# Writing out the loops of a two-layer cross-attention kernel

## What is computed

```
layer 0:  x += cproj(attention_16_heads_of_32(LN(x), ctx, mask))
          x += proj(gelu_tanh(fc(LN(x))))               # 512 -> 2048 -> 512
layer 1:  for i in (1, 2):                               # two attentions, 16 heads of 128
              k, v = ctx @ wk_i + bk_i, ctx @ wv_i + bv_i  # and one extra key and value per head
              x += wo_i(softmax(LN(x) @ wq_i @ k.T / sqrt(128)) @ v)
          x += fc2(gelu(fc1(LN(x))))
```

## Time and profile before

| | us |
|---|---|
| median of three runs | 2413.54 (2409.4 to 2414.35) |
| profiled execution | 2421.03 |
| its span, first to last instruction | 2419.1 |
| PE busy | 2326.3 (96%) |
| PE weight loads busy | 2116.8 (88%) |
| DVE busy | 1343.4 (56%) |
| ACT busy | 1147.9 (47%) |
| POOL busy | 377.6 (16%) |

### The profile page before, as it was taken

One profiled execution on the slowest core, in us unless ns is written; L12 is line 12 of the kernel. 1 busy time (PEld: TensorE's weight loads), 2 busy tenths in 40 slices (PEclk: granted clock), 3 DMA queues, 4 the chain that ended last, 5 costly groups with the idle time before them and its releaser, 6 DMA issues.

```text
span 2419.1 us, 45272 instructions
## 1 busy us (share of the span) xinstructions
PE 2326.3 (96%) x13859; PEld 2116.8 (88%) x13859; DVE 1343.4 (56%) x3154; ACT 1147.9 (47%) x2531; POOL 377.6 (16%) x739
## 2 busy tenths in 40 slices
PE   6899899999999999999999999999999999999999
PEld 5777678888999998999998788999998999998888
DVE  5677774443556555556565524565565565554843
ACT  4677752344445444445444444454454454443421
POOL 4011126430000100100101120001001001002421
PEclk9999989999999999999999999999999999999999
DMA  5322126475455545545645464555555556544110
GB/s 170 119 80 80 58 79 218 174 229 143 160 182 182 179 179 181 180 179 188 197 145 151 161 195 126 182 182 182 197 177 170 197 173 199 198 135 153 57 53 31
DMA packets 232451, 376.32 MB, mean 156 GB/s; under 512 B 57278, under 2 KB 185682, under 8 KB 232258
## 3 DMA queue, kind: packets, MB, share of 16 engines
q1 hardware_dynamic: 232258, 373.87, 46.4%
HBM read 315.77 MB, written 58.05 MB: 155 GB/s over the span
## 4 chain that ended last, share of the span: by engine, by line
PE 83%; issue 7%; DVE 3%; ACT 3%; DMA 2%; POOL 1%; SPq 1%; ACTq 0%; DVEq 0%; POOLq 0%
PE ps_k L1477 9%; PE ps_k L1478 9%; PE ps_k L1479 9%; PE ps_o L1477 8%; PE ps_o L1479 8%; PE ps_o L1478 8%; PE ps_v L1477 5%; PE ps_v L1478 5%; PE ps_v L1479 5%; PE ps_s L1477 4%; PE ps_s L1479 4%; PE ps_s L1478 4%; PE ps_t L1632 3%; PE ps_t L1573 1%; DMA q<-q_scratch 1%
## 5 line engine op out<-in xcount | busy, mean ns | idle before, releaser
L1477 PE MATMUL ps_k<-cs_hi,w_a_hi 128*128 128x376 f32 x1152 | 394.8, 343 | 6.1 <-DVE k_lo L1263 4.3
L1478 PE MATMUL ps_k<-cs_lo,w_a_hi 128*128 128x376 f32 x1152 | 387.9, 337 | 0.0
L1479 PE MATMUL ps_k<-cs_hi,w_a_lo 128*128 128x376 f32 x1152 | 386.7, 336 | 0.0
L970 ACT ACTIVATE prob<-ps_s,row_columns 112x376 f32<-112x376 f32 x256 | 147.2, 575 | 301.6 <-DVE row_columns L1269 301.6
L753 POOL CAST k_hi<-xk_hi 128x1 fp32r x256 | 47.0, 184 | 1290.3 <-PE ps_s L1479 1290.3
L1477 PEld LDWEIGHTS ps_k<-cs_hi,w_a_hi 128*128 128x128 f32 x1152 | 219.5, 191 | 11.2 <-DVE k_lo L1263 8.4
L1478 PEld LDWEIGHTS ps_k<-cs_lo,w_a_hi 128*128 128x128 f32 x1152 | 219.9, 191 | 0.1
L1479 PEld LDWEIGHTS ps_k<-cs_hi,w_a_lo 128*128 128x128 f32 x1152 | 219.0, 190 | 0.0
L1263 DVE SCALAR_TENSOR_TENSOR k_lo<-ps_k,col_b,k_hi 128x375 fp32r<-128x375 f32 x256 | 155.2, 606 | 103.2 <-ACT k_hi L938 98.6
L938 ACT ACTIVATE k_hi<-ps_k,col_b 128x375 fp32r<-128x375 f32 x256 | 146.3, 572 | 107.8 <-PE ps_k L1479 104.9
L717 POOL TENSOR_TENSOR w_b_lo<-w_raw_b,w_b_hi 128x512 fp32r<-128x512 f32 x88 | 120.7, 1400 | 430.6 <-ACT w_b_hi L803 430.6
(11 more groups left out here) (253 smaller groups left out, 5982.7 us busy)
## 6 DMA issues: line engine op xcount, KB each, us to landing
ckd_hi<-context_by_key_halves SPq DMA_DIRECT2D x64, 768.0 KB, 4.3
ckd_lo<-context_by_key_halves SPq DMA_DIRECT2D x64, 768.0 KB, 5.9
cs_hi<-context_halves SPq DMA_DIRECT2D x64, 752.0 KB, 5.9
cs_lo<-context_halves SPq DMA_DIRECT2D x64, 752.0 KB, 7.4
w_raw_b<-in_blocks_b SPq DMA_DIRECT2D x104, 256.0 KB, 3.9
w_raw_a<-in_blocks_a SPq DMA_DIRECT2D x104, 256.0 KB, 4.3
q<-q_scratch SPq DMA_DIRECT2D x72, 224.0 KB, 5.5
shared<-extra_probability SPq DMA_DIRECT2D x32, 448.0 KB, 4.7
```

What stands on the lines that cost most here:

```text
L970: act.activation(prob[buf][0:LQ, 0:KW], ps_s[buf][0:LQ, 0:KW], ACT.Exp, bias=max_neg[0:LQ, buf:buf + 1], accum_out=prob_sum[0:LQ, buf:buf ...
L1477: pe.matmul(out, w_h, m_h, start=first, stop=False)
L1478: pe.matmul(out, w_h, m_l, start=False, stop=False)
L1479: return pe.matmul(out, w_l, m_h, start=False, stop=last)
```

## The change

All engine loops become Python loops, so that every engine's program is written out once from beginning to end, without loop counters and branches. What was computed in registers from a loop variable becomes a constant in the instruction.

```diff
-            with eng.Fori(1, 3) as fg:
+            for fg in range(1, 3):
                 mlp(0, fg, 1, RT * (fg + 1))
             mlp(0, 3, 1, RT * 4, norm=2)
-            with eng.Fori(0, 2) as a:
+            for a in range(0, 2):
                 ln(2 + a, 5 * RT + 4 * RT * a)
                 contexts(ATT1, a)
...
             pair_of(ATT0, 0, 0, 0, one_batch)
-            with eng.Fori(1, PAIRS - 1) as p:
+            for p in range(1, PAIRS - 1):
                 pair_of(ATT0, 0, 0, p, one_batch)
             pair_of(ATT0, 0, 0, PAIRS - 1, one_batch, True)
...
                 pair_of(ATT1, a, group, 0, one_batch)
-                with eng.Fori(1, PAIRS - 1) as p:
+                for p in range(1, PAIRS - 1):
                     pair_of(ATT1, a, group, p, one_batch)
...
-            with eng.Fori(1, GROUPS - 1) as group:
+            for group in range(1, GROUPS - 1):
                 block(group)
             block(GROUPS - 1, True)
```

## The result

The changed kernel takes 2399.13 us (median of 7 runs, 2397.17 to 2401.91) against 2413.54 us of the kernel before (7 runs beside it, 2406.03 to 2415.62): ratio 0.9942, 95% interval 0.9930 to 0.9953, so 14.0 us less (11 to 17). The forecast was 2390.6 in a range of 2381 to 2404: right in sign and inside the range, with 60% of the gain that was forecast. On the profiled executions it is 2421.03 to 2401.91 us, 19.1 less.

A forecast was written before the change was run, and what follows sets the result against it. TensorE's matmuls, in flight 2326.3 of 2419.1 us, were taken as the bound. Terms of 9.3 + 10.0 + 0 + 2.6 + 1.0 = 22.9 us, off the timed 2413.54, gave 2390.6 us, range 2381 to 2404.

The forecast's parts named there:

- (1): The two returns of L337 (a = 0 and 1): 9.3 us won, bounds 8.7 and 10.9.
- (2): The return of L293, ahead of the queries of a = 1: 10.0 us won, bounds 4.0 and 11.1.
- the staging wait: At about 1400 PE waits for ACT, whose staging tile is held by queued q stores: 0.4 us of new wait.
- (3): The eight other returns (L330 six, L323 and L290 one each): nothing won, bounds 0 and 1.8 us.
- (4): Register arithmetic: 1.8 us won in the attention prologues and 0.8 in layer 0's batches; bounds 0 and 5.
- (5): SP's arithmetic before it issues the q loads: 1.0 us won, bounds 0 and 7.2.
- (6): The longer program, in which each instruction is read once: cost taken at 0.
- The rival on straight-line misses: Straight-line reading misses code pages in the attention: slower, 2436 us with 15 missed pages; chance 0.05.
- the one on stalls that exist only under the profiler: Stalls occur only while the profiler records, or fetches move past the old return: no gain, 2413.5 us; chance 0.06.
- I carry the saving over in full: The whole 22.9 us saving, reckoned on the profiled execution, was taken off the timed median 2413.54, giving 2390.6.
- its two pages: The skill's rule that a taken branch outside two held pages forces a fetch: 42 us, 2372, no chance of its own.

The follow-up runs named there:

- the last experiment: The changed kernel with SP's load of the next queries put ahead of the eight weight loads: 2387.37 us, ratio 0.9882 against the kernel before.
- loops of one pass: The kernel before with each pass of every loop made a loop of its own, so no engine goes back: 2400.13 us, ratio 0.9935.
- padded: The changed kernel with idle semaphore increments at the start (100 on PE, 64 each on ACT and DVE): 2414.25 us, ratio 0.9993.
- the two with only ACT padded: The kernel before with 64 or 128 idle semaphore increments on ACT ahead of its first wait: 2412.15 us (0.9996) and 2414.69 us (1.0006).
- the padded kernels: Idle semaphore increments on PE, ACT and DVE at the start of the kernel before (2436.66 us, 1.0088) and of the changed kernel (2414.25 us, 0.9993).

## Why the prediction was right, and where it was too high

By its own steps, on the profiled scale (22.9 us forecast, 19.1 measured):

(1) L337: forecast 9.3, bounds 8.7 and 10.9; measured 4.0 + 5.0 = 9.0 (6.6 + 5.0 with group 1 of a = 0 taken in, as above). The reading that this is fetching behind a long return holds: it goes with both long loops written out, short loops kept, and comes back with L337 kept alone.

(2) L293: forecast 10.0, bounds 4.0 and 11.1; measured 8.1. The clock came back to 1.00 as forecast, and the staging wait behind it is there with 0.5 us. Both executions are the longest of their kind. The same stretch takes 353.5 to 358.9 us in the five kernels that keep the return of L293, and 345.3 to 350.8 in the seven that don't.

(3) The eight short returns: 0, and 0 measured, above all by the kernel that kept only these.

(4) Register arithmetic: 2.6, and this term failed in the larger of its two parts. The prologue's 1.8 did not come. PE waits 5.6 us for `k_lo` against 4.3, and a round lasts as long as before (from one making of `k_lo` at L1263 to the next, 591.75 to 595.55 us before and 592.68 to 596.48 after, 3.80 both times). Many of the register operations had carried the semaphore waits; with them gone a semaphore instruction stands in their place (ACT 1262 instead of 1100, DVE 539 instead of 461). Why the round keeps its length beyond this is not shown. Layer 0's 0.8 did come, and more: about 1.5 us, in every kernel that writes it out. By the run that kept the short loops, these loops and their arithmetic together are worth 1 us, give or take 5.

(5) q: forecast 1.0; PE's waits for it are 10.8 us against 9.6. q stands behind weights in the DMA engines, as the prediction said, and faster issues do not move it; another order does (the last experiment).

(6) The longer program: 0 as forecast. No wait of PE in issue behind the start in four straight kernels (the changed one, loops of one pass, q earlier, padded). The rival on straight-line misses is refuted by them, and so is the one on stalls that exist only under the profiler.

The rest of the miss is one of scale. "I carry the saving over in full" was the step that failed by most: 2421.03 was 7.5 us above the median, and in the changed kernel the profiled execution is 2.8 above, which is 4.7 of the 8.5 us between 2390.6 and 2399.13. With more runs one sees what this was. In the ten experiments the profiled execution is one of the timed runs, and lies anywhere from 4.5 us below their median to 3.5 above. So 7.5 us was mostly the scatter of a single execution, and no constant cost of profiling that a second kernel would share. The kernel before spreads from 2405.7 to 2422.8 over 76 runs in all. PE's fetch behind the same return takes now more and now less (its branch of L293 4.9 us in the kernel before, 3.4 and 3.5 in the two with only ACT padded, where PE's instructions are the same), so it is likely, and not shown, that the profiled execution was one in which the returns were dear.

The other 3.8 us are terms: 0.3 in (1), 1.9 in (2), 2.6 in (4) and 1.0 in (5) too high, and 1.0 lost ahead of layer 1, which hides there what layer 0 gave. Against these stand 2.6 won in group 1 of a = 0, whose batch at q's wait took 22.8 us instead of 24.4, and 0.4 in group 1 of a = 1 (175.9 to 175.5). So the sum owes part of its nearness to luck: terms that didn't come were in part made up by a shorter wait for q in group 1. That isn't the change: with the old loops and only ACT padded, the same group took 175.2 and 175.5 us.

What I had not foreseen is that the parts don't add. The prediction priced each return by itself, and the sum came out; but with the groups' loop left in place the whole price stays (15.7 us for two returns, 14.0 for three). That writing out the attentions moves the groups' code, and so changes which engines miss, fits the padded kernels, and no run shows it by itself.

The Trainium skill (Runtime: NRT & Kernel Launch, section Instruction fetch mechanics) gives PE room for 2048 instructions and the other engines for 512; I had worked only with its two pages. By these sizes PE's short bodies (about 600 instructions between branches of L330) stay in reach, and the trace agrees. PE's body of L337, 1806 instructions, is under 2048 and misses by 3.3 to 3.8 us each time; ACT's, 352, is under 512 and misses or not by its place. So the trace disagrees with the size as the only condition.

## What to carry to other kernels

Read the branches by line before unrolling: a return is worth writing out only where its branch, or the first instruction behind it on any engine, stalls (here 3 of 11). Then time the whole, and don't judge by one loop: writing out the attentions alone gave nothing here, and with the groups 13 us, because code that moves can change the price of the returns left (9 us for the same instructions in the padded kernels). Price a return by the matmuls behind it as well as by the stall: with the same stalls of PE a batch took 3.6 us more in one kernel than in another, 3.1 of it at the lower clock. Don't carry one profiled execution's distance from the median over to another kernel. And where batches have plain numbers, their loads can be ordered batch by batch, which was worth as much again.

## What the runs showed of the hardware

- ACT's stall behind a return of the same loop came with 64 more instructions ahead and went with 128.
- With PE's own stalls behind a return alike, the batch's 119 matmuls kept it busy 21.2 us at a granted clock of 1.00 and 24.3 at 0.87.
- A semaphore increment in a row takes about 150 ns on PE and 70 to 77 on ACT, though its record lasts 51 and 17 ns.
- A branch that isn't taken costs PE 67 to 92 ns behind a full queue, and nothing that shows in the time.
- One profiled execution lay from 4.5 us below to 7.5 above the median of its kernel.
